# Running sums over rows of 16 edges held in one PSUM bank, in a four-layer graph network

## The reference, cut to what matters

```
# layer 0: attention weights alpha over edges of one dst
msg   = softmax(en * r_feat * alpha, axis=-1)          # (E, 2, 32)
g_sum = segment_sum(msg, dst).sum(axis=1)              # (N, 32)
# layer 1: plain sum of the source rows
out   = segment_sum(h[src], dst)
# layer 2: messages from an edge network and the source rows
agg   = segment_sum(messages(h[src], edge_sh, edge_radial), dst) / 4
# layer 3: four-head attention, summed over src
```

## Time and profile before

| what | us |
|---|---|
| median of 3 runs (11333.13 to 11340.17) | 11337.2 |
| the profiled execution's own time | 11342.38 |
| its span in the profile | 11340.5 |
| POOL busy (72% of the span) | 8172.6 |
| DVE busy (57%) | 6446.3 |
| PE busy (31%) | 3495.2 |
| ACT busy (29%) | 3246.1 |
| gather and count stage, first to last POOL command (L901) | 89.1 to 2213.4 |
| sorting stage (L1103) | 2363.9 to 4456.3 |
| plain-sum stage (L1353) | 4627.4 to 6609.0 |
| products stage (L1353) | 6771.6 to 8815.1 |
| attention stage (L1912) | 9144.3 to 11141.7 |

### The profile page before, as it was taken

One profiled execution on the slowest core, in us unless ns is written; L12 is line 12 of the kernel. 1 busy time (PEld: TensorE's weight loads), 2 busy tenths in 40 slices (PEclk: granted clock), 3 DMA queues, 4 the chain that ended last, 5 costly groups with the idle time before them and its releaser, 6 DMA issues. The chain is left out here.

```text
span 11340.5 us, 94121 instructions
## 1 busy us (share of the span) xinstructions
PE 3495.2 (31%) x22342; PEld 2355.7 (21%) x22342; DVE 6446.3 (57%) x10384; ACT 3246.1 (29%) x5001; POOL 8172.6 (72%) x8498
## 2 busy tenths in 40 slices
PE   3201100056666663000000008878878200000002
PEld 2200100055555553000000003333333100000002
DVE  8748865698888885200000018888888334444442
ACT  0012221145555553111111102222222023334331
POOL 5777777657777777777777767777777577777775
PEclk6555555578888886555555558888888555555555
DMA  7124433211111111111111111111111112222222
GB/s 259 52 85 133 133 111 103 88 53 66 66 56 66 57 65 36 31 26 26 26 26 26 26 35 27 28 29 29 27 29 28 24 44 71 71 71 71 71 71 59
DMA packets 462695, 680.58 MB, mean 60 GB/s; under 512 B 263781, under 2 KB 359878, under 8 KB 424630
## 3 DMA queue, kind: packets, MB, share of 16 engines
q0 software_dynamic: 270016, 149.13, 8.4%
q10 hardware_dynamic: 67072, 346.84, 8.1%
q1 hardware_dynamic: 125558, 184.07, 4.8%
HBM read 368.75 MB, written 310.60 MB: 60 GB/s over the span
## 5 line engine op out<-in xcount | busy, mean ns | idle before, releaser
L1353 POOL DMA_INDIRECT hs<-tab_h,idx x3136 | 3030.0, 966 | 1034.5 <-issue 996.9
L1103 POOL DMA_INDIRECT by_src<-ends,pos_i x1568 | 1578.7, 1007 | 664.3 <-issue 510.1
L1912 POOL DMA_INDIRECT hs<-tab_h,idx x1568 | 1479.9, 944 | 518.8 <-issue 518.8
L901 POOL DMA_INDIRECT en<-tab_s,idx x1568 | 1488.8, 949 | 500.3 <-issue 462.9
L615 DVE COPY fresh<-run 128x32 f32<-128x32 f32 (+1 forms) x392 | 101.0, 258 | 1791.0 <-ACT fresh L1437 1776.6
L1571 PE MATMUL tp_ps<-w_pair,x 128*128 128x512 f32 x1568 | 907.0, 662 | 6.2 <-DVE prod_b L1711 6.2
L625 DVE TENSOR_TENSOR_SCAN run<-keep,fresh 128x544 f32<-128x544 f32 (+1 forms) x392 | 851.3, 2172 | 60.0 <-DVE fresh L615 37.9
L954 PE MATMUL cnt_ps<-hot_hi,hot_lo 128*128 128x98 bf16 x3136 | 287.3, 281 | 1853.0 <-DVE hot_hi L979 1853.0
L639 ACT COPY rows<-run 128x512 f32<-128x512 f32 (+1 forms) x392 | 707.3, 1804 | 223.2 <-DVE run L625 223.2
L1798 PE MATMUL turn<-ident,both 128*33 128x128 f32 x8 | 1.9, 422 | 2163.5 <-DVEq L1828 2163.5
L1124 PE MATMUL rank_ps<-place_sb,hot_t 128*128 128x98 f32 x3136 | 646.2, 317 | 60.8 <-DVE picked L1254 60.3
(11 more groups left out here) (341 smaller groups left out, 13045.0 us busy)
## 6 DMA issues: line engine op xcount, KB each, us to landing
sums<-rows ACTq DMA_DIRECT2D x49, 2176.0 KB
sums<-rows ACTq DMA_DIRECT2D x147, 512.0 KB
hs<-tab_h,idx POOLq DMA_INDIRECT x4704, 2.4
ev_rows<-zeros ACTq DMA_DIRECT2D x16, 3136.0 KB
en_rows<-en SPq DMA_DIRECT2D x49, 1024.0 KB, 4.2
en_back<-en_rows ACTq DMA_DIRECT2D x49, 1024.0 KB
raw<-ev_rows ACTq DMA_DIRECT2D x49, 1024.0 KB, 5.0
en<-en_rows SPq DMA_DIRECT2D x49, 1024.0 KB
```

The source lines that it names most:

```text
L901: pool.indirect_dma_start(en[s][:, g, :], None, tab_s0, bass.IndirectOffsetOnAxis(ap=idx[s][:, g:g + 1], axis=0)).then_inc(gathered[s], 16)
L1103: pool.indirect_dma_start(by_src, bass.IndirectOffsetOnAxis(ap=pos_i[k][:, g:g + 1], axis=0), ends[k][:, g, :], None).then_inc(sent[k], 16)
L1353: pool.indirect_dma_start(rows[k][:, g, :], None, tab_h, bass.IndirectOffsetOnAxis(ap=idx[k][:, g:g + 1], axis=0)).then_inc(gathered[k], 16)
L1912: pool.indirect_dma_start(rows[k][:, g, :], None, tab_h3, bass.IndirectOffsetOnAxis(ap=idx[k][:, g:g + 1], axis=0)).then_inc(gathered[k], 16)
```

## The change

A new class `RowSums` takes the place of `SegmentSums` in the sorting, plain-sum and products stages. A feature's row is exactly 16 edges, so `fresh` has 32 x 16 = 512 numbers, which is one PSUM bank. In all three stages `fresh` lies in PSUM, in one bank for both chunks, in the plain-sum stage in one bank for each. Column 0 now is the first edge's message. `carry` multiplies the last column of the run before by that edge's flag into `so_far` (SBUF), and the new `begin` adds `so_far` to the first column of `fresh` before the scan. To free a bank in the sorting stage, the turned rows and the counts share one (`turn_bank`), so that PE's `turn` also waits for ACT's copy of the counts, and the counts' product waits for ACT's copies of the turned rows.

```diff
+        class RowSums:
+            def __init__(self, st, table, buffers=1):
+                fresh = [ps(st, f"fresh{k}", [EP, FEAT, CH]) for k in range(buffers)]
+                self.fresh = [fresh[k % buffers] for k in range(2)]
+                self.keep = [sb(st, f"keep{k}", [EP, FEAT, CH]) for k in range(2)]
+                self.run = [sb(st, f"run{k}", [EP, FEAT, CH]) for k in range(2)]
+                self.so_far = sb(st, "so_far", [EP, FEAT])
...
+            def mask(self, act, t, k):
+                K.wait(act, "act", self.scanned, t - 1)
+                flags = by_dst.cont[:, bass.ds(t * CH + 1, CH - 1)].unsqueeze(1).to_broadcast([EP, FEAT, CH - 1])
+                nc.scalar.copy(self.keep[k][:, :, 1:CH], flags).then_inc(self.kept, 1)
+
+            def carry(self, c, t, k):
+                return c.mark(nc.vector.tensor_tensor(self.so_far[:, :], self.run[1 - k][:, :, CH - 1],
+                                                      by_dst.cont[:, bass.ds(t * CH, 1)].to_broadcast([EP, FEAT]), ALU.mult))
+
+            def begin(self, c, k):
+                return c.mark(nc.vector.tensor_tensor(self.fresh[k][:, :, 0], self.fresh[k][:, :, 0], self.so_far[:, :], ALU.add))
+
+            def scan(self, dve, t, k, settle=True):
+                K.wait(dve, "dve", self.kept, t + 1, self.copied, t - 1)
+                flat = lambda ap: ap[:, :, :].rearrange("p f c -> p (f c)")
+                nc.vector.tensor_tensor_scan(flat(self.run[k]), flat(self.keep[k]), flat(self.fresh[k]), 0.0,
+                                             ALU.mult, ALU.add).then_inc(self.scanned, 1)
+                if settle:
+                    K.wait(dve, "dve", self.scanned, t + 1)
...
 # sorting stage
-            place_ps = ps(st, "place_ps", [NP, NB])
-            turn_ps = ps(st, "turn_ps", [NP, GR, 128], BF16)
+            turn_bank = ps(st, "turn_bank", [NP, 512])
+            turn_ps = turn_bank[:, 0:GR * 64].bitcast(BF16).rearrange("p (g e) -> p g e", g=GR)
+            place_ps = turn_bank[:, 384:384 + NB]
-            S = SegmentSums(st, FEAT, sums)
+            S = RowSums(st, sums)
...
-                    K.wait(pe, "pe", turned_sb, n)
+                    K.wait(pe, "pe", turned_sb, n, place_out, n)
...
-                            K.wait(pe, "pe", place_out, n + 1)
+                            if q < GROUPS - 1 or not known_ge(t, last_chunk):
+                                K.wait(pe, "pe", place_out, n + 1, turned_sb, n + 2)
+                            else:
+                                K.wait(pe, "pe", place_out, n + 1)
...
-                    c.link(nc.vector.tensor_reduce(S.message(k), ..., AX.X, ALU.add))
-                    S.scan(dve, c, t, k, carried=True)
+                    c.step(nc.vector.tensor_reduce(S.message(k), ..., AX.X, ALU.add))
+                    c.until(S.begin(c, k))
+                    S.scan(dve, t, k)
...
 # plain-sum stage
-            S = SegmentSums(st, FEAT, sums, psum=2)
+            S = RowSums(st, sums, buffers=2)
...
+                        S.carry(c, t, k)
                         K.wait(dve, "dve", laid, t + 1)
-                        S.scan(dve, c, t, k)
+                        c.join()
+                        c.until(S.begin(c, k))
+                        S.scan(dve, t, k)
...
 # products stage
-            S = SegmentSums(st, FEAT, sums)
+            S = RowSums(st, sums)
...
-                    K.wait(act, "act", messaged, t + 1, S.scanned, t - 1)
+                    K.wait(act, "act", messaged, t + 1, S.scanned, t)
...
                                     K.wait(dve, "dve", laid, t)
-                                    S.scan(dve, c, t - 1, 1 - k, carried=True, settle=False)
+                                    c.until(S.begin(c, 1 - k))
+                                    S.scan(dve, t - 1, 1 - k, settle=False)
```

More of the change, by code:

```diff
@@ L645, in finish, with message, start, store @@
                 act.wait_ge(self.stored, 16 * PAIRS)
+        class RowSums:
+            def __init__(self, st, table, buffers=1):
+                self.table, self.buffers = edge_rows(table), buffers
+                fresh = [ps(st, f"fresh{k}", [EP, FEAT, CH]) for k in range(buffers)]
[3 more added lines that the diff above has]
+                self.so_far = sb(st, "so_far", [EP, FEAT])
+                self.rows = sb(st, "rows", [EP, 2 * CH, FEAT])
+                self.kept, self.scanned, self.copied = K.sem("kept"), K.sem("scanned"), K.sem("copied")
+                self.stored = K.sem("stored_pair")
+            def message(self, k):
+                return self.fresh[k][:, :, :]
+            def start(self):
+                for k in range(2):
+                    last = nc.vector.memset(self.keep[k][:, :, 0], 0.0)
+                return [last, nc.vector.memset(self.run[1][:, :, CH - 1], 0.0)]
+            def mask(self, act, t, k):
[14 more added lines that the diff above has]
+                    K.wait(dve, "dve", self.scanned, t + 1)
+            def store(self, act, t, k, i):
+                if k == 0:
+                    K.wait(act, "act", self.scanned, t + 1, self.stored, i * 16)
+                else:
+                    K.wait(act, "act", self.scanned, t + 1)
+                nc.scalar.copy(self.rows[:, k * CH:(k + 1) * CH, :], self.run[k][:, :, :].rearrange("p f c -> p c f")).then_inc(self.copied, 1)
+                if k == 1:
+                    K.wait(act, "act", self.copied, t + 1)
+                    act.dma_start(self.table[:, cols2(i), :], self.rows[:, :, :]).then_inc(self.stored, 16)
+            def finish(self, act):
+                act.wait_ge(self.stored, 16 * PAIRS)
@@ L1151, in body @@
                             last.then_inc(samed, 1)
-                            K.wait(pe, "pe", place_out, n + 1)
-                            nc.tensor.matmul(place_ps[:, :], ident[:, :], place_sb[q][:, :], start=True, stop=False)
+                            if q < GROUPS - 1 or not known_ge(t, last_chunk):
+                                K.wait(pe, "pe", place_out, n + 1, turned_sb, n + 2)
+                            else:
+                                K.wait(pe, "pe", place_out, n + 1)
+                            nc.tensor.matmul(place_ps, ident[:, :], place_sb[q][:, :], start=True, stop=False)
                             for g in range(GR):
-                                last = nc.tensor.matmul(place_ps[:, :], hot_lo[k][:, q * GR + g, :], hot_hi[k][:, q * GR + g, :],
+                                last = nc.tensor.matmul(place_ps, hot_lo[k][:, q * GR + g, :], hot_hi[k][:, q * GR + g, :],
                                                         start=False, stop=g == GR - 1)
@@ L1195, in body @@
                             K.wait(act, "act", placed, n + 1, ranked, n - (GROUPS - 2))
-                            nc.scalar.copy(place_sb[(q + 1) % GROUPS][:, :], place_ps[:, :]).then_inc(place_out, 1)
+                            nc.scalar.copy(place_sb[(q + 1) % GROUPS][:, :], place_ps).then_inc(place_out, 1)
                             if q == 0 and not first_chunk(t):
@@ L1244, in add_up @@
                 def add_up(t, k):
-                    c.link(nc.vector.tensor_reduce(S.message(k), z[k][:, :, :].rearrange("p c (h f) -> p f c h", h=HEADS0), AX.X, ALU.add))
-                    S.scan(dve, c, t, k, carried=True)
+                    c.step(nc.vector.tensor_reduce(S.message(k), z[k][:, :, :].rearrange("p c (h f) -> p f c h", h=HEADS0), AX.X, ALU.add))
+                    c.until(S.begin(c, k))
+                    S.scan(dve, t, k)
                 def pick(n, k, q):
@@ L1295, in body @@
                             divided = divide(1 - k)
-                            S.carry(c, 1 - k)
+                            S.carry(c, t - 1, 1 - k)
                         pick(t * GROUPS + 2, k, 2)
@@ L1308, in _ @@
                 c.until(divide(1))
-                S.carry(c, 1)
+                S.carry(c, last_chunk, 1)
                 add_up(last_chunk, 1)
@@ L1728, in body @@
                         K.wait(dve, "dve", S.scanned, t)
-                        S.carry(c, k)
+                        S.carry(c, t, k)
                         c.until(crossed)
@@ L1736, in _ @@
                 dve.wait_ge(laid, 2 * PAIRS)
-                S.scan(dve, chains[1], 2 * PAIRS - 1, 1, carried=True)
+                c = chains[1]
+                c.until(S.begin(c, 1))
+                S.scan(dve, 2 * PAIRS - 1, 1)
         K.recycle()
```

## The result

The changed kernel takes 11250.57 us (median of 4 runs, 11247.12 to 11260.18) against 11335.17 us for the kernel before in the same comparison: 0.9927 of it, 95% interval 0.991 to 0.9944, or 84.6 us less. 72 us less were forecast. The profiled execution has a span of 11246.5 us where before it was 11340.5, 94.0 us less.

The account below looks back on a forecast made before the run. The prediction took POOL's indirect-DMA count times pitch as the bound. Its terms, -46 (products) - 30 (sorting) + 0 (plain-sum) + 1 (stage ends) + 3 (first chunk) = -72 us, gave 11265 us on the median's footing, whole range 11225 to 11318.

Parts of the forecast that it names:

- The bound and the mechanism: POOL's command count times pitch sets a stage's length; a scan with both inputs in SBUF holds its commands.
- D: Rival: no change, by the skill's inference or because something beside the scan's operands matters; -0 to -10 us, chance 0.05.
- Products stage: Scan out of SBUF frees 96 stretched commands: -46 us, bounds 30 and 63; 17 us or so stay under L1672, L1727, L1731.
- Sorting stage: Scan's hold on 91 commands goes, -42 us; L1272 holds more, +12 us (bounds 17 less, 45 more); together -30 us.
- the random phase: Sorting stage: without the scan's hold L1272 meets POOL at any phase, 0.43 us a chunk, in half of the chunks.
- Rival A: Sorting stage: L1272 meets POOL badly in every chunk, costing 85 instead of 17 us; total -16 to -45, chance 0.14.
- the prediction's sign of being wrong: Sorting stage: the prediction is wrong if L1272 stretches a command in most chunks by over 0.8 us.
- Plain-sum stage: `fresh` is in PSUM before and after, and `carry` on two SBUF tiles is short: 0 us, bounds 0 and +20.
- Cover: DVE's chunk grows about 0.4 us, hidden by its waits: 0.4 us left in products, 2.5 us available in sorting.
- B: Products stage: DVE becomes the bound if `begin` with its wait costs 0.9 us; 5 to 25 us given back, chance 0.09.
- The shared bank: Sorting stage: 0.64 us more a group on PE, hidden, with 3.9 us of PE's wait left; first chunk +3 us.
- C: Rival, sorting stage: PE and ACT in the shared bank stretch PE's part, POOL waits for positions; 11374 us, chance 0.06.

Follow-up runs that it names:

- e3: The changed kernel with only `fresh` moved to SBUF in all three stages: 11365.79 us, 1.0025 of the kernel before.
- e2: The kernel before with the new class and the shared bank in the sorting stage only: 11299.74 us, 0.9966 of the kernel before.
- e5: The changed kernel with the sorting stage's product `en * r` in four pieces, back to back: 11231.49 us, 0.991 of the kernel before.
- e4: The kernel before with only turned rows and counts in one bank and the two waits for it: 11344.66 us, 1.0005 of the kernel before.
- e9: The kernel before with SP's row loads of a pair of chunks issued later, after the placing of the pair before: 11335.39 us, 0.9998.
- e6: The changed kernel with the product `en * r` in four pieces, the last three between DVE's picks: 11227.25 us, 0.9904 of the kernel before.

## Why the prediction came out right, and what it missed

**The bound and the mechanism** held. No command is long under a scan any more. Where one operand of the scan went back to SBUF (e3), the hold came back, in a stage that never had it too. This settles D. What the prediction took from the Trainium skill ("SBUF — State Buffer", section "Who interferes with whom"), that an instruction with at most one SBUF input leaves GpSimd alone, agrees with the 0.96 us under L689 and L1346. The inference of the same section that a `tensor_tensor` with two SBUF inputs doesn't hold up descriptor generation does not agree: L1339 makes a command 1.81 us long, and cut into pieces it gives back 35 of 45 us. The measurement decides. But the prediction left out what that section says just before, that an instruction with two SBUF inputs contends with a GpSimd instruction that reads SBUF. POOL's commands here read their indices (`pos_i`, `idx`) from SBUF, so the measured hold agrees with that sentence. Whether it is this reading that is held up, no run here shows.

**Products stage**, forecast -46: -51.9. All time over 0.944 us a command was 66.3 us and is 14.6. The scan's 46 went as a whole. What DVE's other products cost (L1672, L1727, L1731, and some 1 us under L1673 and L1677, which the prediction didn't name) was 20.0 us, not "17 or so", and 14.6 are left; this gain wasn't in the sum.

**Sorting stage**, forecast -42 + 12 = -30: -38.4, with two terms that were off and partly met. The scan's 42 went. But L1339 holds 77 commands for 45 us, where L1272 held for 17: it took back 28 us, not 12. The step that failed is the random phase, 0.43 us a chunk, that the prediction gave to the half of the chunks that don't start from POOL's landing: about 21 of its 29 us. Told apart by whether DVE waited for that landing in the 21 us before the product:

| chunks | before: number, held us | after: number, held us |
|---|---|---|
| DVE waited for a landing | 49, 9.5 | 42, 9.5 |
| it didn't | 49, 8.3 | 56, 35.7 |

For the chunks with a wait, where about 8 us were left in the prediction's sum, 9.5 came, though not by the working given there: the product falls 16.8 or 17.6 us behind the wait (16.65 or 17.4 before, of which the prediction had the first alone), and only at 16.8 just behind a command's start. The other 56 meet POOL at no random phase. L1339 holds a command in 52 of them, by 0.64 us a chunk, and in 34 by over 0.8 us. Their distances from the chunk before are a few fixed ones, and with them the phase: in 29 of the 56 chunks the product comes 18.7 us behind that of the chunk before, and each of them holds a command by 0.81 to 0.89 us; in 22 it comes 19.4 or 19.5 us behind, with most of them at 0.30 to 0.38. One of the 29, behind a chunk with a wait:

```profile
3001.22 1.22 DVE L1339 TENSOR_TENSOR z<-en,r 128x1024 f32<-128x1024 f32 x1
3001.97 1.30 POOL L1166 DMA_INDIRECT by_src<-ends,pos_i  x1 [0.30 <-issue]
...
3019.90 1.21 DVE L1339 TENSOR_TENSOR z<-en,r 128x1024 f32<-128x1024 f32 x1
3020.13 1.83 POOL L1166 DMA_INDIRECT by_src<-ends,pos_i  x1 [0.30 <-issue]
```

In e3, where the scan holds POOL again, the 51 chunks without a wait hold for 11.8 us only. So the prediction was right that the scan's hold sets the step in which POOL and the product meet, and wrong in taking what comes without it for chance. That 45 us lie near its 42 for a random phase everywhere is a coincidence of 0.23 and 0.64 us a chunk. Rival A was true by some two fifths: it asked for up to 85, 68 more than before, and 28 came; its bad phase is there in 37 of 98 chunks, not in most, so the prediction's sign of being wrong (over 0.8 us in most chunks) didn't show. Commands gained 14 us alone. The other 24.4 us were in no term: DVE's chunk, and with it SP's load, moved against POOL's pauses. This gain comes with the edit (e2 has it too), but not by the mechanism that the edit was made for, and e5 shows how easily a part of it goes again. Without it the change would have brought about 85 - 24 = 61 us; that is worked out, not measured.

**Plain-sum stage**, forecast 0: +0.4. `carry` with two SBUF operands (0.20 us) held nothing: all the commands' time there is that of before. **`begin`**: 0.199 us and its wait, 0.21 us (20.7 / 98), as was taken; the scan takes 1.221 us, where 1.21 was said.

**Cover.** In the products stage DVE waits (76.6 - 21.6) / 96 = 0.57 us a chunk for the gather, where 0.4 were forecast, so B stayed away, but not by much. In the sorting stage DVE waits 171.1 us for POOL.

**The shared bank**: +0.73 us a group (3.65 for 2.92; 0.64 was said), PE's wait for the one-hot rows 380.2 / 91 = 4.2 us a chunk (3.9 was said), first command +2.9 us (+3). e4 shows it at nothing in the time. C's stretching of PE didn't come about, and the clock went the other way: the granted clock of the sorting stage, 0.81 in the earlier trace rows, is 0.85 after, and 0.85 in e4 with the bank alone:

```profile
2514.00:4421.00 1907.00, 1284.78 (x12636) 1127.83 (x12812) 1594.56 (x4380) 1083.20 (x2045) 1450.84 (x1456) 0.85 0.19 62
```

The median fell by 13 us more than forecast, the span by 22: 6 in the products stage, 8 in the sorting stage, 7 in the stretches between stages, which nothing here explains. About 9 of the 22 are only where the two profiled executions lie beside their medians. That the figure came so close is partly luck in the sorting stage: 16 us worse on L1339, 24 better on the pauses. A small slip of the prediction stands apart from this: by its own terms A's better end is -46 + 0 + 1 + 3 = -42 us, not -45.

## What to carry to other kernels

Where GpSimd's indirect DMAs set the length of a stage, look in the timeline for commands of more than their plain length and for what VectorE runs at that moment. Move one of that instruction's two SBUF operands to PSUM, or, where that can't be, cut it into pieces: each piece holds a command only until its own end, and VectorE's longer work must fit into the time in which it waits anyway. When one such instruction is freed, ask at which phase the next one will then meet GpSimd in each chunk: two loops of fixed steps can stay at a bad phase (held in 52 of 56 chunks here), and the mean over all phases is then too kind. And a loop that is bound by one queue has pauses that depend on when other queues issue: look at the time between the commands by itself, before and after, and don't credit it to the mechanism that the edit was made for.

## What the runs showed of the hardware that wasn't expected

- A pause of 1.7 us after every 112th indirect DMA of the sorting stage, at fixed places of the loop: four commands or 109 more on the same queue before it don't move it. The plain-sum and products stages have it behind the same commands (1.5 to 2.1 us in all traces), the attention stage too, there of 4.7 and 2.0 us in turn, the 4.7 each time 4.7 us behind ACT's store.
- That pause is 4.9 to 6.4 us if the large row loads of SP were issued 1.5 to 2.7 us before it begins, in 33 of 33 cases, and 0.8 to 1.9 us if 0.2 to 0.8 us before, in 16 of 16. e9 moved the loads and the long pauses went. That the pause waits for the transfers ahead of it is the reading that fits; what does it wasn't shown.
- A command held by VectorE ends at a fixed distance behind the instruction that holds it, wherever in it it began: a gather 0.75 us behind a scan and 0.79 to 0.83 us behind a `tensor_tensor` of the products stage, the sorting stage's scatter 0.78 us behind a scan and 0.84 to 0.86 us behind the product `en * r`. In the pieces of e6 the next piece, which starts 0.1 us later, doesn't hold it again.
